# Band and probability transfers in halves of 64 rows in a decoder layer with relative positions

## The reference, cut to what matters

```
idx   = clip(pos[None, :] - pos[:, None], -20, 20) + 20
rk2, rv2 = rel_k[idx], rel_v[idx]
attn  = softmax((einsum('bhqd,bhkd->bhqk', q, k) + einsum('bhqd,qkd->bhqk', q, rk2)) / sqrt(16), axis=-1)
x     = einsum('bhqk,bhkd->bhqd', attn, v) + einsum('bhqk,qkd->bhqd', attn, rv2)
```

## Time and profile before

| | |
|---|---|
| median of 3 runs | 3123.89 us |
| profiled execution | 3123.3 us, span 3121.5 us |
| PE (TensorE) busy | 2691.9 us, 86% |
| DVE (VectorE) busy | 1772.3 us, 57% |
| ACT (ScalarE) busy | 1219.7 us, 39% |
| POOL (GpSimd) busy | 1295.8 us, 42% |
| bytes moved by DMA | 270.72 MB, mean 87 GB/s |

### The profile page before, as it was taken

How to read it: one execution, slowest core, us unless ns; L and a number is a source line. 1 busy time by engine, 2 the same in 40 slices (tenths; PEclk the granted TensorE clock), 3 DMA queues, 4 the chain that set the end, 5 groups by cost and what they waited for, 6 DMA issues and landing times.

```text
span 3121.5 us, 51792 instructions
## 1 busy us (share of the span) xinstructions
PE 2691.9 (86%) x15346; PEld 1844.6 (59%) x15346; DVE 1772.3 (57%) x4053; ACT 1219.7 (39%) x2184; POOL 1295.8 (42%) x1038
## 2 busy tenths in 40 slices
PE   3687899788997899878997899978998889978998
PEld 2465566555665656555665556656575656655565
DVE  5746545666456654665456564656546664565636
ACT  1237223453235423362234532364234622354323
POOL 2543344424434244433444254343444344342544
PEclk8899899989999899998999999999999989998999
DMA  8518001860048300780028500582007800394006
GB/s 241 123 33 196 29 0 49 179 157 1 7 99 194 86 1 7 166 188 25 1 57 184 144 1 7 114 195 69 1 15 168 202 1 1 78 193 114 1 7 135
DMA packets 487136, 270.72 MB, mean 87 GB/s; under 512 B 218619, under 2 KB 482644, under 8 KB 483540
## 3 DMA queue, kind: packets, MB, share of 16 engines
q1 hardware_dynamic: 449636, 260.78, 34.6%
q10 hardware_dynamic: 37152, 5.90, 1.9%
HBM read 136.11 MB, written 130.50 MB: 85 GB/s over the span
## 4 chain that ended last, share of the span: by engine, by line
PE 63%; DMA 10%; DVE 8%; issue 8%; SPq 5%; ACT 4%; POOL 2%; ACTq 0%; DVEq 0%; POOLq 0%
PE PS L1574 58%; DMA prob_scr<-arena 9%; PE PS L1577 5%; SPq L599 1%; ACT arena L1084 1%; DVE arena L479 1%; SPq L587 1%; ACT arena L1091 1%; SPq L578 1%; POOL rstd L429 1%; SPq L682 1%; DVE arena L1284 0%; DVE qrc L453 0%; DVE arena L477 0%; DVE cbn L1251 0%
## 5 line engine op out<-in xcount | busy, mean ns | idle before, releaser
L1574 PE MATMUL PS<-arena 128*17 128x128 f32 (+6 forms) x6864 | 806.7, 316 | 141.7 <-ACT arena L1084 127.6
L1574 PEld LDWEIGHTS PS<-arena 128*17 128x17 f32 (+3 forms) x6864 | 542.1, 127 | 347.3 <-ACT arena L1084 164.1
L1577 PE MATMUL PS<-ident,arena 128*128 128x128 f32 x3362 | 541.8, 290 | 106.3 <-DVE arena L1277 39.7
L1577 PEld LDWEIGHTS PS<-ident,arena 128*128 128x128 f32 x3362 | 406.7, 148 | 295.4 <-issue 143.6
L1356 DVE CUSTOM_DVE_ANT_0 PS<-PS,arena 128x512 f32<-128x512 f32 x512 | 346.4, 707 | 230.5 <-DMA arena<-bias_scr 138.1
L1574 PE MATMUL PS<-cwk,arena 128*128 128x512 f32 (+1 forms) x936 | 470.5, 627 | 2.7 <-ACT arena L977 2.7
L429 POOL TENSOR_TENSOR crn<-crn,mhalf 128x8 f32<-128x8 f32 (+1 forms) x234 | 419.3, 1798 | 123.8 <-DVE crn L1265 122.1
L1084 ACT ACTIVATE arena<-PS,nmax 128x512 f32<-128x512 f32 x512 | 344.3, 700 | 205.6 <-DMA prob_scr<-arena 145.3
L972 ACT ACTIVATE arena<-PS 128x512 f32<-128x512 f32 (+1 forms) x234 | 139.6, 597 | 683.5 <-PE PS L1574 683.5
L869 POOL TENSOR_TENSOR arena<-arena,mass_mask 128x512 f32<-128x512 f32 x128 | 163.8, 1280 | 410.1 <-ACT arena L1084 391.1
L1574 PEld LDWEIGHTS PS<-cwk,arena 128*128 128x128 f32 (+1 forms) x936 | 181.6, 199 | 147.1 <-issue 133.1
(11 more groups left out here) (161 smaller groups left out, 3684.6 us busy)
## 6 DMA issues: line engine op xcount, KB each, us to landing
arena<-bias_scr SPq DMA_DIRECT2D x130, 336.0 KB, 4.4
prob_scr<-arena SPq DMA_DIRECT2D x128, 336.0 KB, 4.9
bias_scr<-arena SPq DMA_DIRECT2D x132, 256.0 KB, 5.4
q_scr<-arena SPq DMA_DIRECT2D x144, 128.0 KB
arena<-q_scr SPq DMA_DIRECT2D x132, 128.0 KB, 5.5
arena<-k_scr SPq DMA_DIRECT2D x18, 768.0 KB, 12.1
arena<-prob_scr SPq DMA_DIRECT2D x128, 80.0 KB, 4.1
arena<-far_scr SPq DMA_DIRECT2D x18, 546.0 KB, 7.5
```

The lines of the kernel that those rows point to most:

```text
L1574: return pe.matmul(o, l, r, start=start, stop=stop, **kw)
L1577: return pe.transpose(o, i, ident[0:i.shape[0], 0:i.shape[0]])
```

## The change

It moves windows and probabilities in two halves of 64 rows. Half i needs only the columns from 64 i to 64 i + 103, so a row has 104 floats in place of 168, and the row pitch of the scratch falls to 105 and 104. Each `load_window` and `store_probs` is then two DMAs, and its semaphore counts 32 in place of 16. The triangle is 64 columns wide in place of 128. What the narrower windows leave out is written in the tile: the left square of the lower half is zero for good and is zeroed once a turn, and the right square of the upper half is the far value, which GpSimd writes for each group (`fill_far`, after `edge_mass`). `load_band` is issued two groups behind its store in place of one. The diff, cut to its core:

```
+HP = 64
+HWIN = HP + BAND
-SKEW = WIN + 1
+SKEW = HWIN + 1
-EQ = HG * 128
+EQ = HG * HP
...
+        def half_rows(scr, t, g, i):
+            return scr[t, g * HG:(g + 1) * HG, i * HP * SKEW:i * HP * SKEW + HP * HWIN].rearrange("h (p r) -> p h r", r=HWIN)
...
-                sp.dma_start(Wn[:, (g % 2) * HG:(g % 2 + 1) * HG, 0:WIN],
-                             bias_scr[t, g * HG:(g + 1) * HG, 0:128 * WIN]
-                             .rearrange("h (p r) -> p h r", r=WIN)).then_inc(win_loaded[g % 2], 16)
+                for i in range(2):
+                    sp.dma_start(Wn[i * HP:(i + 1) * HP, (g % 2) * HG:(g % 2 + 1) * HG, i * HP:i * HP + HWIN],
+                                 half_rows(bias_scr, t, g, i)).then_inc(win_loaded[g % 2], 16)
...
-                    sp.dma_start(prob_scr[t, g * HG:(g + 1) * HG, 0:128 * WIN].rearrange("h (p r) -> p h r", r=WIN),
-                                 P[:, (g % 2) * HG:(g % 2 + 1) * HG, t * 128:t * 128 + WIN]).then_inc(p_stored[g % 2], 16)
+                    for i in range(2):
+                        at = t * 128 + i * HP
+                        sp.dma_start(half_rows(prob_scr, t, g, i),
+                                     P[i * HP:(i + 1) * HP, (g % 2) * HG:(g % 2 + 1) * HG, at:at + HWIN]).then_inc(p_stored[g % 2], 16)
...
                         store_probs(t, g)
-                        if g:
-                            load_band(t, g - 1)
+                        if g > 1:
+                            load_band(t, g - 2)
+                        elif t:
+                            load_band(t - 1, g + NG - 2)
...
-                    load_band(t, NG - 1)
+                    if last:
+                        load_band(t, NG - 2)
+                        load_band(t, NG - 1)
...
-                pool.tensor_tensor(Eb[:, eb_slot(t, g), :, :], tail_mask[:].unsqueeze(1).broadcast_to([128, HG, 128]),
-                                   bcast(Rb[:, t, g * HG:(g + 1) * HG, BAND], 128), ALU.mult).then_inc(eb_ready, 1)
+                pool.tensor_tensor(Eb[:, eb_slot(t, g), :, :], tail_mask[:].unsqueeze(1).broadcast_to([128, HG, HP]),
+                                   bcast(Rb[:, t, g * HG:(g + 1) * HG, BAND], HP), ALU.mult).then_inc(eb_ready, 1)
...
+            def margins(nb, g):
...
                 pool.memset(Wn[:, g * HG:(g + 1) * HG, WIN:WP], 0.0).then_inc(margins_zero, 1)
+                pool.wait_ge(margins_zero, 5 * nb + (2 if g == 0 else 4) + 1)
+                pool.sem_inc(waits_alone, 1)
+                pool.memset(Wn[HP:128, g * HG:(g + 1) * HG, 0:HP], 0.0).then_inc(margins_zero, 1)
+                pool.wait_ge(margins_zero, 5 * nb + (3 if g == 0 else 5) + 1)
+                pool.sem_inc(waits_alone, 1)
+                fill_far(nb, 0, g)
+
+            def fill_far(nb, t, g):
+                m = (nb * T + t) * NG + g
+                if t or g > 1:
+                    pool.wait_ge(scores_biased, (m - 1) * HG + 1)
+                    pool.sem_inc(waits_alone, 1)
+                    pool.wait_ge(mass_mul, m)
+                    pool.sem_inc(waits_alone, 1)
+                pool.tensor_copy(Wn[0:HP, (g % 2) * HG:(g % 2 + 1) * HG, HWIN:WIN],
+                                 bcast(Rb[0:HP, t, g * HG:(g + 1) * HG, BAND], HP)).then_inc(far_filled, 1)
+                pool.wait_ge(far_filled, m + 2)
+                pool.sem_inc(waits_alone, 1)
...
                         edge_mass(t, g)
+                        if g + 2 < NG:
+                            fill_far(b, t, g + 2)
+                        elif t + 1 < T:
+                            fill_far(b, t + 1, g + 2 - NG)
...
                     if j == 0:
-                        dve.wait_ge(win_loaded[g % 2], 16 * (tile * 2 + g // 2 + 1) + 1)
+                        dve.wait_ge(win_loaded[g % 2], 32 * (tile * 2 + g // 2 + 1) + 1)
+                        dve.wait_ge(far_filled, tile * NG + g + 2)
```

More of the change, by code:

```diff
@@ L118, in build @@
         ident = sb("ident", [128, 128])
-        tail_mask = sb("tail_mask", [128, 128])
+        tail_mask = sb("tail_mask", [128, HP])
         mass_mask = sb("mass_mask", [128, 128])
@@ L190, in build @@
         Qrest, Krest = xn.rearrange("p t e -> p (t e)").rearrange("p (c s) -> p c s", c=2), KT
-        Eb = carve(4 * EQ, (4 * EQ,), ot_at).rearrange("p (k h c) -> p k h c", k=4, c=128)
+        Eb = carve(4 * EQ, (4 * EQ,), ot_at + 1024).rearrange("p (k h c) -> p k h c", k=4, c=HP)
         Rb = carve(T * H * NREL, (T, H, NREL), band_at)
@@ L328, in build @@
         far_part = sem("far_part")
+        far_filled = sem("far_filled")
         win_loaded = [sem("win_loaded0"), sem("win_loaded1")]
@@ L586, in store_eb @@
                 sp.sem_inc(waits_alone, 1)
-                sp.dma_start(bias_scr[t, g * HG:(g + 1) * HG].rearrange("h (p r) -> p h r", r=SKEW)[:, :, BAND:BAND + 128],
+                sp.dma_start(bias_scr[t, g * HG:(g + 1) * HG].rearrange("h (p r) -> p h r", r=SKEW)[:, :, BAND:HWIN],
                              Eb[:, eb_slot(t, g), :, :]).then_inc(eb_stored[g], 16)
@@ L675, in store_probs @@
                     sp.sem_inc(waits_alone, 1)
-                    sp.dma_start(prob_scr[t, g * HG:(g + 1) * HG, 0:128 * WIN].rearrange("h (p r) -> p h r", r=WIN),
-                                 P[:, (g % 2) * HG:(g % 2 + 1) * HG, t * 128:t * 128 + WIN]).then_inc(p_stored[g % 2], 16)
+                    for i in range(2):
+                        at = t * 128 + i * HP
+                        sp.dma_start(half_rows(prob_scr, t, g, i),
+                                     P[i * HP:(i + 1) * HP, (g % 2) * HG:(g % 2 + 1) * HG, at:at + HWIN]).then_inc(p_stored[g % 2], 16)
                 def load_band(t, g):
-                    sp.wait_ge(p_stored[g % 2], 16 * ((b * T + t) * 2 + g // 2 + 1) + 1)
+                    sp.wait_ge(p_stored[g % 2], 32 * ((b * T + t) * 2 + g // 2 + 1) + 1)
                     sp.sem_inc(waits_alone, 1)
@@ L708, in _ @@
                 sp.sem_inc(waits_alone, 1)
-                sp.wait_ge(p_stored[1], 16 * T * 2 * (b + 1) + 1)
+                sp.wait_ge(p_stored[1], 32 * T * 2 * (b + 1) + 1)
                 sp.sem_inc(waits_alone, 1)
@@ L731, in _ @@
             for k in range(2):
-                sp.wait_ge(win_loaded[k], 16 * (T * 2 * NB + 1) + 1)
+                sp.wait_ge(win_loaded[k], 32 * (T * 2 * NB + 1) + 1)
             for g in range(NG):
@@ L799, in last_far @@
                 pool.tensor_tensor(far_of(nb)[1][2], far_of(nb)[0], far_of(nb)[1][1], ALU.subtract).then_inc(far_ready, 1)
-            def margins(g):
+            def margins(nb, g):
                 if g == 0:
@@ L850, in _ @@
             pool.wait_ge(m_act, 4 + 1)
-            margins(0)
-            margins(1)
+            margins(0, 0)
+            margins(0, 1)
             pads(0)
@@ L944, in _ @@
                 pool.sem_inc(waits_alone, 1)
-                margins(0)
+                margins(b + 1, 0)
                 finish(3)
-                margins(1)
+                margins(b + 1, 1)
                 far_edge(b + 1, 0, 2)
@@ L1079, in exps @@
                         act.wait_ge(mass_mul, m)
-                        act.wait_ge(p_stored[g % 2], 16 * (tile * 2 + g // 2) + 1)
+                        act.wait_ge(p_stored[g % 2], 32 * (tile * 2 + g // 2) + 1)
                     if t == 0 and h == 0:
@@ L1380, in attn_dve @@
                             edge_sum(t, h // HG)
-                dve.wait_ge(margins_zero, 3 * (b + 1) + 1)
+                dve.wait_ge(margins_zero, 5 * (b + 1) + 1)
                 dve.sem_inc(waits_alone, 1)
@@ L2032, in _arrange @@
     d["ident"] = np.eye(128, dtype=f)
-    d["tail_mask"] = (np.arange(128)[None] < 128 - p).astype(f)
+    d["tail_mask"] = (np.arange(HP)[None] < HP - p % HP).astype(f)
     c = np.arange(128)[None] + MAX_REL
```

## The result

The changed kernel took 3099.46 us (median of 4 runs, 3096.6 to 3100.75) where the kernel before took 3122.62 us beside it: ratio 0.9924, interval 0.9907 to 0.9941, so about 0.8% or 23 us faster. The forecast was 3025 us. The kernel before itself took 3123 to 3166 us from one comparison to the next, which ran on several chips; so every kernel is given as its ratio to the kernel before that ran beside it. Where two such ratios come from different comparisons, a difference of 0.3% between them says nothing, since the changed kernel's own two ratios are that far apart.

What follows compares the result with a forecast made beforehand. Late DMA transfers, with no engine full and SP waiting at `load_band`, were taken to bound attention. From 3123.3 us, 91 came off for stretches of 76.0 in place of 87.4 and 8 for turn ends: 3025 us, range 2960 to 3105.

Steps and rivals of the forecast that it cites:

- The place: The eight attention stretches, 87.4 us each, where no engine is full; forecast to fall to 76.0 us, 91 us in all.
- The wait for the band: SP's 15.9 us a stretch in front of `load_band`, forecast to go, letting windows and stores out earlier.
- Bytes: In a stretch 5.5 MB of 16.52 go; at 0.037 ns a byte DMA engine time falls 12.9 us, to 59.1.
- Landings: Time for stored probabilities to land in attention: 5.4 us in the median before, forecast 4.5 us.
- the loop of `P`: Reuse of a `P` buffer every second group: exponentials, SP's issue and landing, 8.8 us for two groups, 4.4 a group.
- Two more issues a group: SP's list in attention, seven issues in place of five: 0.53 us each, 4.2 us a group with semaphore waits.
- SP's queue is last: Slower rival: SP's list sets each attention group and two new issues come on top, 3161 us; chance 0.05.
- The band stores: Two stores of 320 KB between attention groups; with stalled issues they were given 0.3 us a group.
- `fill_far`: GpSimd's copy for each group, 0.40 us, forecast hidden behind `edge_sum`; if not, at most 0.4 us a group, 51 in all.
- End of a turn: Two shorter `far_edge` before `quant_finish` save 1 us a turn; 7.6 us taken off in all, with `margins` growing.
- the cover of 1.9 us: Time from the end of the last `quant_finish` to PE's transposes, expected to hide about 1.1 us of longer `margins`.
- Short stores: Slower rival: short-row stores in attention cost a second access, 26.1 us more engine time a stretch, 3244 us; chance 0.05.

## Why the prediction was wrong

- *The place was right.* Attention was what moved, and the rest of a turn stayed to 0.4 us in 1922.
- *The wait for the band* went as said, and the list did the rest: 1.5% by itself.
- *Bytes.* Forecast 12.9 us of engine time less in a stretch, from 72.0 to 59.1. Measured 63.4 us, or 61.9 with whole transfers: 9 to 10 us less than the kernel before. Against the whole transfers with the bands two groups behind, which have the old bytes and 76.3 us, it is 14.4 us less. The same packets took 72.0, 76.3 and 83.0 us by how they were issued, so a fixed price of a packet, on which the sum rests, is not what these runs show. The size of the term was fair; the bytes' gain, 2.0%, is there.
- *Landings.* Forecast 4.5, measured 2.9 us. That would have made the loop of `P` 3.6 us a group, so this term was too careful.
- *Two more issues a group: the step that failed.* I took 0.53 us for one more issue, read from issues of 128 rows, and 4.2 us for a group's list, which therefore stayed below the 4.4 us of the loop of `P` and dropped out of the sum. An issue of 64 rows takes 0.57 us at least and 0.61 in the median, and with what lies between the issues the list takes 4.9 to 6.3 us, 5.6 in the median, about 0.8 us an issue. So the list is last, and not the landings. I had this as a rival, "SP's queue is last", which turns at 0.78 us an issue, at a chance of 0.05. Its condition came true and its time, 3161 us, did not: it put the new issues on top of groups of 5.46 us in which SP had in truth been waiting, 15.9 us a stretch, for the band. The price of the halved rows, measured by leaving them out, is 2.5 to 2.8%, 77 to 88 us, about the whole miss of 75. In the profiles 8 x (83.8 - 75.5) = 66 us of it lie in the attention, where the forecast missed by 8 x (83.8 - 76.0) = 62.
- *The band stores* had 0.3 us a group in my sum, together with stalls. With the late list they make two groups of 8 to 10 us of every 16; cutting them up gives 1.0% on halves. They are no new cost of the change: the kernel before had them too, and its longest groups took 7 to 9 us by the starts of their exponentials. The forecast of 4.7 us for every group had no room for them. The two terms overlap: with whole transfers of 104 columns the bursts stay and 75.5 us are reached all the same, so their price depends on how fast SP catches up behind one.
- *`fill_far`* is hidden inside the turns, as said; outside, at the first attention, it costs about 2 us once (4.2 us later, of which 2.2 lie ahead of GpSimd's part), which I had not counted.
- *End of a turn.* The 7.6 us for the shorter triangles did not show in the time. `quant_finish` (L489) now waits for the fill ahead of it; timeline of POOL, then of PE:
```profile
1295.34 1.39 POOL L489 TENSOR_TENSOR arena<-arena,qsc 128x704 f32<-128x704 f32 x1 [0.34 <-POOL arena L833]
```
```profile
1297.50 0.88 PE L1614 MATMUL PS<-ident,arena 128*128 128x128 f32 x6
```
It ends at 1296.73, 0.8 us before PE's turn, so the cover of 1.9 us held and shrank to 0.8. The trace suggests where the microsecond of the triangles went. Two of the seven stretches between attentions, of the changed kernel and then of the kernel before, chosen for the same busy time of PE and the same granted clock, 0.96 in the third column from the right:
```profile
1388.10:1660.60 272.50, 248.47 (x1051) 169.38 (x1050) 145.22 (x314) 82.64 (x146) 118.81 (x97) 0.96 0.20 46
2463.30:2736.00 272.70, 248.52 (x1051) 169.41 (x1050) 145.27 (x315) 82.70 (x147) 118.79 (x97) 0.96 0.20 45
```
```profile
1402.60:1676.00 273.40, 248.61 (x1051) 169.47 (x1050) 145.21 (x315) 82.70 (x147) 119.11 (x93) 0.96 0.21 49
2126.10:2399.40 273.30, 248.49 (x1051) 169.47 (x1050) 145.19 (x314) 82.65 (x146) 119.06 (x93) 0.96 0.21 49
```
At the same clock these stretches are 0.6 to 0.9 us shorter, near the 1 us forecast. But four of the changed kernel's seven stretches were granted 0.94 or 0.95, the kernel before had one such, and PE was busy for 8.4 us more in sum (1755.51 against 1747.09). Whether the lower clock belongs to the change or to these two executions was not tried.
- *Short stores are not dear here.* The rival did not come: the kernel whose stores have 416 and 256 bytes a row, in whole transfers, was 2.0% faster than the one with 672 and 512. The Trainium skill (DMA: Bandwidth & Descriptors, Specifications) has 512 bytes as the least for line rate, with read-modify-write below. No extra cost of that kind shows in these times; the gain per byte, smaller than in proportion (11.36 MB in place of 16.52 take 63.4 us in place of 72.0), is all that could be read that way.

## What to carry to other kernels

An issue is work on the issuing queue: before a transfer is split to save bytes, add up the list of its queue for one turn of the loop and set it against the turn, with the issue duration of the new shape, not of the old one. A queue can be the bound while it waits for nobody, and its list can be longer than the sum of its issues (the shortest group here took 4.9 us with 3.8 us of issues in it); look at whether anyone waits for what it issues. First take out waits in the list and cut up large bursts, which here gave 2.8% with two small edits, before changing the layout. Read the length of a list from several turns of the loop, not from the shortest.

## What the runs showed of the hardware

- An issue of a DMA with 64 rows took 0.574 us at least, with 128 rows 0.359 us, at 416 and 672 bytes a row alike; half the packets did not make it shorter.
- The same packets and bytes took the DMA engines 76.3 us a stretch in transfers of 128 rows x 4 heads, 73.9 in transfers of 128 rows x 2 heads, and 83.0 in transfers of 64 rows x 4 heads.
- 2048 packets of 160 bytes landed after 7.9 us in a stretch where loads of 256 packets landed after 3.0, and the window issued right behind them was first used 7.7 us after its issue (1318.16 to 1325.89).
- At the head of its hardware loop SP's queue stood for 3.0 to 4.2 us in each turn of the kernel before, and for 8.0 to 9.1 us when two such transfers had been issued right ahead of the jump.
- The kernel before differed by 1.4% between comparisons, run on several chips (medians of 3123 to 3166 us), more than between its runs in any one of them (0.8% at most); the ratio of the changed kernel held within 0.33%.
